# Two MoE layers: rows sorted by expert through DRAM and multiplied in fixed blocks of 128, in place of every listed expert over every row

## What is computed

```python
x = x + 0.5 * L0_ffn(layernorm(x))     # an adapter picked for each sequence
x = x + L0_attn(layernorm(x))
x = x + 0.5 * L0_ffn(layernorm(x))
x = x + 0.5 * L1_ffn(layernorm(x))     # MoE, the first
x = x + L1_attn(layernorm(x))          # selective scan
x = x + 0.5 * L1_ffn(layernorm(x))     # MoE, the second
```

```python
scores = sigmoid(xf @ gate_w + bias)
top_scores, top_idx = top_k(scores, 2)
top_scores = top_scores / (top_scores.sum(-1) + 1e-6)
w = zeros((T, 8)); w[t, top_idx] += top_scores
hact = gelu(einsum('th,ehi->tei', xf, up_w) + up_b)
eo = einsum('tei,eih->teh', hact, down_w) + down_b
combined = einsum('teh,te->th', eo * 0.1, w)
shared = (gelu(xf @ sw_up + sb_up) @ sw_down + sb_down) * 0.1
out = shared + combined
out = out / (max(abs(out), -1) + 1e-6)
```

## Time and profile before

| | |
|---|---|
| median of 3 runs | 1553.57 us (1551.65 to 1554.36) |
| the profiled execution, its own time | 1552.47 us |
| its span in the trace | 1550.7 us |
| PE busy | 1394.1 us, 90% |
| DVE / ACT / POOL busy | 947.5 / 801.6 / 400.0 us |
| mean granted clock of TensorE | 0.946 of 2.4 GHz |
| first MoE layer, from its first instruction to the barrier behind it | 664.1 to 965.5 us |
| second MoE layer, from its first instruction to the end | 1260.0 to 1550.7 us |

### The profile page before, as it was taken

One profiled execution on the slowest core, in us unless ns is written; L12 is line 12 of the kernel. 1 busy time (PEld: TensorE's weight loads), 2 busy tenths in 40 slices (PEclk: granted clock), 3 DMA queues, 4 the chain that ended last, 5 costly groups with the idle time before them and its releaser, 6 DMA issues. The chain is left out here.

```text
span 1550.7 us, 22874 instructions
## 1 busy us (share of the span) xinstructions
PE 1394.1 (90%) x7314; PEld 729.1 (47%) x7314; DVE 947.5 (61%) x1896; ACT 801.6 (52%) x1465; POOL 400.0 (26%) x585
## 2 busy tenths in 40 slices
PE   2896899999999879799999997899998779999997
PEld 1672222222222257567777764122221157777776
DVE  5677688889889347451222256699899941222236
ACT  0220688888888714354343354665666444443432
POOL 4021232322330012220000002788888710000000
PEclk9996799999999979889999998799999979999999
DMA  4020121222211010000000000444444300000001
GB/s 94 0 83 1 62 73 52 63 72 72 79 66 43 1 19 1 1 16 1 17 16 1 17 1 23 159 157 140 146 133 154 111 1 16 16 15 2 16 14 42
DMA packets 81206, 77.31 MB, mean 50 GB/s; under 512 B 21004, under 2 KB 60376, under 8 KB 81112
## 3 DMA queue, kind: packets, MB, share of 16 engines
q1 hardware_dynamic: 78992, 75.85, 15.7%
q10 hardware_dynamic: 2120, 0.28, 0.2%
HBM read 55.78 MB, written 16.78 MB: 47 GB/s over the span
## 5 line engine op out<-in xcount | busy, mean ns | idle before, releaser
L1375 ACT ACTIVATE m_hidden<-m_pU,m_up_b 128x512 f32<-128x512 f32 x320 | 219.8, 687 | 265.6 <-PE m_pU L1524 265.4
L1183 DVE TENSOR_REDUCE at_nm<-at_mx 128x2 f32<-128x1024 f32 x256 | 303.8, 1219 | 40.4 <-PE at_mx L1026 39.0
L1531 PEld LDWEIGHTS m_pD<-m_down,m_hidden 128*128 128x128 f32 x2560 | 296.7, 192 | 32.5 <-issue 32.5
L1531 PE MATMUL m_pD<-m_down,m_hidden 128*128 128x128 f32 x2560 | 297.1, 275 | 0.0
L1129 ACT ACTIVATE at_probs<-at_ring 128x512 f32<-128x512 f32 x512 | 269.2, 605 | 47.3 <-PE at_ring L1038 45.8
L1524 PE MATMUL m_pU<-m_xT_all,m_up 128*128 128x512 f32 x640 | 291.2, 601 | 1.1 <-PEq L305 0.5
L1500 DVE TENSOR_TENSOR m_out_b<-m_pD,m_down_b 128x512 f32<-128x512 f32 x64 | 44.2, 691 | 288.6 <-PE m_pD L1531 288.6
L1524 PEld LDWEIGHTS m_pU<-m_xT_all,m_up 128*128 128x128 f32 x640 | 118.0, 193 | 123.7 <-issue 123.5
L2023 POOL TENSOR_TENSOR ss_hc<-ss_h,ss_c_all 128x512 f32<-128x512 f32 x128 | 161.9, 1271 | 52.1 <-DVE ss_h L2195 44.6
L1038 PE MATMUL at_ring<-at_qq,at_kk 51*128 51x512 bf16 x512 | 163.3, 386 | 7.1 <-ACT at_probs L1129 6.1
L1026 PE MATMUL at_mx<-at_kk,at_qq 48*128 48x512 bf16 x512 | 156.0, 398 | 12.7 <-DVE at_nm L1183 8.1
(11 more groups left out here) (282 smaller groups left out, 1511.1 us busy)
## 6 DMA issues: line engine op xcount, KB each, us to landing
ss_dtb<-ss_dt_rows SPq DMA_DIRECT2D x128, 256.0 KB
at_qq<-q_stack SPq DMA_DIRECT2D x64, 96.0 KB, 2.3
at_kk<-k_stack SPq DMA_DIRECT2D x64, 96.0 KB, 2.3
q_stack<-at_qs SPq DMA_DIRECT2D x8, 384.0 KB, 2.6
k_stack<-at_ks SPq DMA_DIRECT2D x8, 384.0 KB, 3.0
ss_stack<-ss_parts SPq DMA_DIRECT2D x96, 32.0 KB, 2.7
X<-in_L_attn_x_dram SPq DMA_DIRECT2D x8, 256.0 KB, 6.1
q_stack<-at_qs SPq DMA_DIRECT2D x8, 256.0 KB, 2.9
```

The costliest lines, as they stand in the source:

```text
L1183: dve.tensor_reduce(nm[group % 2][:, 2 * (pair % 2) + parity, 2 * half:2 * half + 2], mx[parity][:, :, :], AX.X, ALU.max, negate=True).the ...
L1375: act.activation(hidden[t % 2][:, k, :], pU[k][:, :], ACT.Gelu, bias=up_b[buf][:, k:k + 1]).then_inc(s.gelu_done, 1)
L1531: last = pe.matmul(pD[t % 2][:, c, :], hidden[t % 2][:, k, c * P:(c + 1) * P], down[buf][:, k, :], start=(k == 0), stop=(k == NI - 1))
```

## The change

In each MoE layer the shared expert stays as it is. The listed experts go. In their place:

- **Routing.** The chain (now 37 links) gives each of the 8192 pairs a place in a list sorted by half of the sequences (0 to 3, 4 to 7), then by expert, each expert's part padded to a multiple of 128 rows. PE counts with two products after the shared expert's second up product. `index` holds the places, `expert_of` the expert of each block.
- **Scatter.** ACT keeps all normalised rows of the layer in `mw_rows` (130 words: the row, its id, its weight). POOL writes them to DRAM (`sorted_rows`) with indirect DMAs, 128 rows of 520 bytes each: 16 for each half and each choice k, 64 in a layer. Between the choices it waits until the first has landed and sets the id and weight of the other (`mark`).
- **Blocks.** 39 blocks of 128 rows for each half, 78 in a layer, whatever the routing (4096 pairs of a half and at most 8 x 127 of padding). SP loads a block to `xb` (8 buffers). PE transposes it (`turn`), ACT copies the transpose to SBUF (`take_turned`), DVE copies the up weights of the block's expert from `up_all` into one of two fixed places (`take_up`), PE makes four products of 128 columns (`block_up`), ACT four Gelus of 128 columns, PE four products for the down part with weights addressed by a register (`block_down`), DVE adds the bias, multiplies by the row's weight and converts the row ids. POOL writes the 128 results with an indirect DMA (`put`) to `pair_rows` in DRAM, 78 in a layer; padding rows have an id out of bounds and are skipped.
- **Finish.** SP reads both results of a sequence back, DVE adds them to `acc` (now the same memory as `m_xT_all`) and finishes as before. The first half's four sequences are finished during the second half's blocks, in five pieces each from block 47 on (`FINISH_AT`, `PIECES`); the other four after the last block.
- All 8 experts' weights are loaded at the start of the layer (16 DMAs, 4 MB). Each engine that addresses by expert loads the block's expert number into a register (`expert_at`), once a block. Early in the kernel, SP fills both sorted lists in DRAM with empty rows (`fill_sorted`, two DMAs of 9984 rows of 520 bytes). A barrier pair with a clearing of semaphores stands between the first MoE layer and the scan, in addition.

The core of the diff (new sides, with what the text below speaks of):

```diff
+HALVES = 2
+ID, WEIGHT = D, D + 1
+PAIR_ROWS = 2 * NB * L
+HB = (2 * HT * P + E1 * (P - 1)) // P
+TB = HALVES * HB
+X_BUFS, Y_BUFS, T_BUFS = 8, 12, 3
+LEAD_AT = {14: 3, 19: 4, 22: 5, 25: 6, 28: 7, 36: 8, 38: 9}
+SILU_AT = 23
+def fill_sorted(sp, r):
+    sp.wait_ge(r.made, 2)
+    for rows in r.sorted:
+        sp.dma_start(rows.rearrange("(j p) d -> p j d", p=P), r.empty[:, :].unsqueeze(1).broadcast_to([P, TB, ROW])
+                     ).then_inc(r.filled, 16)
...
+            def load_block(j):
+                if j >= X_BUFS:
+                    sp.wait_ge(s.y_ready, j - X_BUFS + 1)
+                sp.dma_start(xb[:, j % X_BUFS, :], sorted_rows[j * P:(j + 1) * P, :]).then_inc(xb_in[j % X_BUFS], 16)
+            def wait_written(blocks):
+                for i in range(Y_BUFS):
+                    sp.wait_ge(y_out[i], 16 * len(range(i, blocks, Y_BUFS)))
...
+            for e in range(E1):
+                sp.dma_start(up_all[:, e, :], ins["L1_ffn_up_w"][e]).then_inc(s.experts_in, 16)
+                sp.dma_start(down_all[:, e, :, :], ins["L1_ffn_down_w"][e].rearrange("(k i) h -> i k h", i=P)
+                             ).then_inc(s.experts_in, 16)
+            sp.wait_ge(s.list_ready, 1)
+            for half in range(HALVES):
+                for k in range(2):
+                    sp.wait_ge(scattered[half][k], 16 * HT)
+                for j in range(HB):
+                    load_block(half * HB + j)
+                    if half and j in Y_LOAD_AT:
+                        if j == min(Y_LOAD_AT):
+                            wait_written(HB)
+                        for b in Y_LOAD_AT[j]:
+                            load_results(b)
+            if lead is not None:
+                scan_lead_stores(sp, lead)
...
+            def mark(half, k):
+                tiles = slice(half * HT, (half + 1) * HT)
+                pool.tensor_copy(v.rows[:, tiles, ID:ROW], v.idw[:, k, tiles, :]).then_inc(s.marked, 1)
+                pool.wait_ge(s.marked, 2 * half + k + 1)
+            def scatter(half, k, t):
+                at_tile = half * HT + t
+                pool.indirect_dma_start(sorted_rows, bass.IndirectOffsetOnAxis(ap=index[:, k, at_tile:at_tile + 1], axis=0),
+                                        v.rows[:, at_tile, :], None, bounds_check=TB * P - 1, oob_is_err=False
+                                        ).then_inc(scattered[half][k], 16)
+            def put(j):
+                pool.wait_ge(s.y_ready, j + 1)
+                pool.indirect_dma_start(pair_rows, bass.IndirectOffsetOnAxis(ap=y_id[j % Y_BUFS][:, :], axis=0),
+                                        y[j % Y_BUFS][:, :], None, bounds_check=PAIR_ROWS - 1, oob_is_err=False
+                                        ).then_inc(y_out[j % Y_BUFS], 16)
+            pool.wait_ge(s.weighted, 1)
+            mark(0, 0)
+            pool.wait_ge(s.placed, 1)
+            for t in range(HT):
+                scatter(0, 0, t)
+            pool.wait_ge(scattered[0][0], 16 * HT)
+            mark(0, 1)
+            for t in range(HT):
+                scatter(0, 1, t)
+            mark(1, 0)
+            for t in range(HT):
+                scatter(1, 0, t)
+            pool.wait_ge(scattered[1][0], 16 * HT)
+            mark(1, 1)
+            for j in range(HB):
+                if j < HT:
+                    scatter(1, 1, j)
+                put(j)
+            for j in range(HB):
...
+            def take_turned(j):
+                act.wait_ge(s.turned, j + 1)
+                if j >= T_BUFS:
+                    act.wait_ge(s.bup_done, j - T_BUFS + 1)
+                act.copy(xT[j % T_BUFS], pU[2 + j % 2][:, 0:P]).then_inc(s.xT_taken, 1)
+            def gelus(j, e):
+                if j >= T_BUFS:
+                    act.wait_ge(s.bdown_done, j - T_BUFS + 1)
+                act.wait_ge(s.bup_done, j + 1)
+                for k in range(NI):
+                    act.activation(hid[j % T_BUFS][:, k, :], pU[j % 2][:, k * P:(k + 1) * P], ACT.Gelu,
+                                   bias=v.up_b[:, bass.ds(e, 1), k:k + 1].rearrange("p a b -> p (a b)")
+                                   ).then_inc(s.hid_done, 1)
+            for j in range(TB):
+                after = expert_at(act, j + 1) if j + 1 < TB else None
+                gelus(j, e)
+                e = after
+                if j + 2 < TB:
+                    take_turned(j + 2)
+                if lead is not None and j - HB in LEAD_AT:
+                    scan_lead_act(act, g, q=ahead, s=lead, t=LEAD_AT[j - HB])
...
+            def finish(b, piece):
+                tiles = slice(b * NC, (b + 1) * NC)
+                if piece == 0:
                     norm.begin(b)
+                    dve.wait_ge(y_in[b % 2], 32 * (b // 2 + 1))
+                    norm.link(dve.tensor_tensor(acc[:, tiles, :], acc[:, tiles, :], yb[b % 2][:, 0, :, :], ALU.add))
+                if piece == 1:
+                    dve.tensor_tensor(acc[:, tiles, :], acc[:, tiles, :], yb[b % 2][:, 1, :, :], ALU.add
+                                      ).then_inc(s.y_added, 1)
+                    dve.wait_ge(s.y_added, b + 1)
+                if piece == 2:
                     norm.link(dve.tensor_reduce(most[:, tiles], acc[:, tiles, :], AX.X, ALU.max,
...
+            def take_up(j, e):
+                if j > 1:
+                    dve.wait_ge(s.bup_done, j - 1)
+                dve.tensor_copy(up_now[j % 2], up_all[:, bass.ds(e, 1), :].rearrange("d a i -> d (a i)")
+                                ).then_inc(s.up_ready, 1)
+            for j in range(TB):
+                if j + 2 < TB:
+                    further = expert_at(dve, j + 2)
+                    take_up(j + 2, further)
+                if j >= Y_BUFS:
+                    dve.wait_ge(y_out[j % Y_BUFS], 16 * (j // Y_BUFS))
+                dve.wait_ge(xb_in[j % X_BUFS], 16 * (j // X_BUFS + 1))
+                dve.tensor_copy(y_id[j % Y_BUFS][:, :], xb[:, j % X_BUFS, ID:ID + 1])
+                dve.wait_ge(s.bdown_done, j + 1)
+                dve.tensor_tensor(yt[j % 2][:, :], pD[j % 2][:, 0, :],
+                                  v.down_b[:, bass.ds(e, 1), :].rearrange("p a d -> p (a d)"), ALU.add
+                                  ).then_inc(s.y_taken, 1)
+                dve.wait_ge(s.y_taken, j + 1)
+                dve.tensor_scalar(y[j % Y_BUFS][:, :], yt[j % 2][:, :], xb[:, j % X_BUFS, WEIGHT:ROW], None, ALU.mult
+                                  ).then_inc(s.y_ready, 1)
+                e, after = after, further
+                jj = j - HB - FINISH_AT
+                if 0 <= jj < HS * PIECES:
...
+            def turn(j):
+                pe.wait_ge(xb_in[j % X_BUFS], 16 * (j // X_BUFS + 1))
+                if j > 1:
+                    pe.wait_ge(s.xT_taken, j - 1)
+                pe.transpose(pU[2 + j % 2][:, 0:P], xb[:, j % X_BUFS, 0:D], g.identf[:, :]).then_inc(s.turned, 1)
+            def block_up(j):
+                pe.wait_ge(s.up_ready, j + 1)
+                pe.wait_ge(s.xT_taken, j + 1)
+                if j > 1:
+                    pe.wait_ge(s.hid_done, NI * (j - 1))
+                for k in range(NI):
+                    last = pe.matmul(pU[j % 2][:, k * P:(k + 1) * P], up_now[j % 2][:, k * P:(k + 1) * P],
+                                     xT[j % T_BUFS], start=True, stop=True)
+                last.then_inc(s.bup_done, 1)
+            def block_down(j, e):
+                pe.wait_ge(s.hid_done, NI * (j + 1))
+                if j > 1:
+                    pe.wait_ge(s.y_taken, j - 1)
+                for k in range(NI):
+                    last = pe.matmul(pD[j % 2][:, 0, :], hid[j % T_BUFS][:, k, :],
+                                     down_all[:, bass.ds(e, 1), k, :].rearrange("i a d -> i (a d)"),
+                                     start=(k == 0), stop=(k == NI - 1))
+                last.then_inc(s.bdown_done, 1)
+            pe.wait_ge(s.experts_in, EXPERT_LOADS)
+            pe.wait_ge(s.list_ready, 1)
+            pe.wait_ge(s.gelu_done, NI * NB)
+            pe.wait_ge(s.shared_acc, NB)
+            e = expert_at(pe, 0)
+            turn(0)
+            turn(1)
+            block_up(0)
+            for j in range(TB):
+                if j + 2 < TB:
...
+            nc.all_engine_barrier()
+            nc.clear_and_free_semaphores(taken_once)
+            nc.all_engine_barrier()
```

592 lines of the change are left out of this document (318 added, 274 removed).

## The result

The changed kernel took 1512.6 us (1509.7 to 1520.4), the kernel before 1553.4 beside it: ratio 0.9746, 95% interval 0.9706 to 0.9787. The prediction was 1514. The profiled execution spans 1508.1 us against 1550.7.

A forecast was written before the change was run, and what follows sets the result against it. PE's columns in the listed experts were taken as the bound. First layer -22.5 us, second -24.6, less added costs, made -40 from 1552.5: 1512.5, and 1.1 more against the median, 1514; range 1460 to 1600.

The forecast's parts named there:

- the terms added at the end of the sum: Outside the layers' sums: second barrier pair 3 us, PE idle then below full clock 1.5 a layer, added constants 1.
- The shared expert, ended at 58: Start of each MoE layer: the shared expert still ends 58 us after the layer's start; PE's routing wait next to nothing.
- POOL's DMA, c = 1.2: POOL's scatters: each indirect DMA costs c = 1.2 us, 32 precede the first block, which starts at 64.4 us.
- the formula: First block starts at 26 + 32c us after the layer's start; the buffer stall adds 48c, together 80 us per us of c.
- The round, 2.1: Each block's round takes 2.1 us, near PE's floor of 1.96; 78 rounds make 164 us a layer.
- finish, 12 us in blocks 47 to 66: Finish pieces on DVE lengthen rounds to 2.9, 2.9 and 3.5 us: 3.0 a sequence, 12 for four, PE waiting for up weights.
- The stall for buffers, 1 us: Block 27 waits for result 15's buffer, held by POOL's scatters: 57.6 against 56.7, so 1 us lost at c = 1.2.
- The lead, 10.5, in the first layer: The scan's start, mixed into the first layer's listed experts, costs 10.5 us there, as before the change.
- The tail, 7 us to the first sum: After the last block: last result, DMA, landing and reading back 7 us, then four sequences 15 us, 19 in the first layer.
- The fills, at nothing: Early in the kernel, two DRAM fills take all DMA engines 61 us but are covered; uncovered they would cost up to 30.
- The rival of the lock: In rounds, DVE's copy waits 0.6 us for POOL's put in 57%: round 2.4, 1561 us; within the long-round rival's 0.13.
- POOL as the bound: Rival, chance 0.26: slower, as start and buffers cost 80 us a layer per us of c over 1.2; 1578 at 1.6.

The follow-up runs named there:

- r9: The changed kernel itself, run again unedited on a held-back chip: 1603.6 us, ratio 1.034.
- e10: Changed kernel with POOL waiting for the landing of each of the 48 scatters ahead of the first put; on the chip of r9: 1733.5 us.
- e1: Changed kernel without DVE's copy of a block's up weights (output not the reference's), on a clean chip: 1490.4 us.
- e6: Changed kernel with DVE loading the expert number into its register one round earlier, on a clean chip: 1502.2 us.
- c1: Changed kernel with 18 result buffers, DVE's register load one round ahead and the lead's stores behind the last reading back; on the chip of r9: 1594.4 us.
- e4: Changed kernel with 18 buffers for results instead of 12, on a clean chip: 1501.8 us.
- e7: Changed kernel with SP issuing the scan lead's stores behind the reading back of the last four sequences, on a held-back chip: 1609.0 us.
- c2: Changed kernel with c1's edits (14 buffers) and, in the first layer, POOL clearing a tile before scatters and the first 39 blocks' puts; clean chip: 1539.7 us.

## Why the prediction was right, and where its steps were not

The number is right on the chips that do not hold PE back, and there partly by luck. The first layer gained 11.5 us where 22.5 were predicted, the second 27.7 where 24.6 were, and the rest of the kernel gained 3.4 where the terms added at the end of the sum were to cost 7. These errors of 11, 3 and 10 us cancel to 2.5. That the result came to such a chip was luck as well: on the chip of r9 the same prediction is wrong. The main path is as predicted: what is saved is PE's columns, and the first block and the blocks' rounds take their time from POOL's issues and from PE.

- **The shared expert, ended at 58.** It ended at 60.9 and 61.1. The two counting products, put at nothing, hold PE for 1.8 us (671.50 to 673.33), and the up products ahead of them took 1.0 longer than before (9.78 against 8.81). This is hidden: the first block comes later still.
- **POOL's DMA, c = 1.2.** 1.275 (0.97 and 0.30 to the next). Shown by POOL's timeline. The first block's transpose came at 66.3 after the start, predicted 64.4; with the c of the trace the formula gives 66.8, and it held within 2.1 us in the first layers at 1.68 and 3.05 (3.7 in e10's second); on a held-back chip at 1.275 it does not hold, 91.3 us in r9. The Trainium skill's "DMA: Bandwidth & Descriptors", "Anatomy of one DMA — SWDGE (gpsimd) path", with 2.0 us for each and most of it landing, stands: a put lands 2.3 us after its issue in the median, and issues follow one another sooner.
- **The round, 2.1.** Too long: 1.89 to 1.90, even under the floor of 1.96. Sixteen half products at 0.112 are right (0.89 and 0.90), but a transpose holds PE for 0.11, not 0.17. On PE the register load and the address steps are hidden altogether, and e1 shows that the copy is too. Rounds 4 to 22 of the second layer have a mean of 1.96 all the same, and 1.90 both in e6 and in e1, so DVE's load and copy together cost some 0.06. In all this gave 11 to 16 us a layer (78 x 0.14 to 78 x 0.2).
- **finish, 12 us in blocks 47 to 66.** Right in the second layer: 2.97, 2.57 and 3.04 are 2.9 over three quiet rounds, 11.5 for four sequences. e6 and e1 show the mechanism: the pieces delay the register load and the copy behind it. With the load moved away (e6, c1) 2.0 of these 2.9 remain, which are the pieces themselves.
- **The stall for buffers, 1 us.** Too small: 6.5 and 6.4. The mechanism was right and the size was not. The inputs account for more than was missing: 48 x 0.075 = 3.6 for c, and blocks that are 0.2 us shorter each reach block 27 some 5.4 us earlier, which gives 10 where 6.5 were waited. So the formula overshoots by 3.5. e4 removed the stall.
- **The lead, 10.5, in the first layer.** Here a step failed: 78 blocks took 184.6 us, first to last transpose, and in the second layer 165.1. Of the 19.5 between them 10.5 were predicted. Some 3 to 4 more are statistics, which I had put into the tail alone: for the first two sequences, where a variance of seven small operations follows them, the rounds are 3.88 and 3.92 us where the second layer has 1.90, and PE waits 1.72 and 1.31 us in them for the copy behind. Those of the other two (0.94 each) fall into rounds in which PE does not wait for DVE. The other 16 or so are the lead itself, half as much again as priced: rounds of 4.47, 3.96, 4.66, 5.72 and 5.85 stand where the second layer has 2.99, 1.97, 2.98, 1.97 and 1.90. In the longest PE waits for ACT's Gelus, which stand behind eight of the lead's operations and two table loads (887.42 to 895.05):

```profile
896.35 2.07 PE L1753 MATMUL m_pD<-m_down_all,m_hidden 128*128 x8 [2.82 <-ACT m_hidden L1531]
```

The POOL work of the lead adds to it at the end. DVE's and POOL's timelines of the kernel after:

```profile
906.20 2.00 DVE L1667 COPY m_up<-m_up_all 128x512 f32 x1 [0.46 <-issue]
...
908.50 1.99 DVE L1688 TENSOR_SCALAR m_y<-m_yt,m_xb 128x128 f32<-128x128 f32 x1
```

```profile
906.62 1.28 POOL L1926 TENSOR_TENSOR ss_corr<-ss_nd,ss_rw 128x512 f32<-128x512 f32 x1
908.07 1.01 POOL L1478 DMA_INDIRECT pair_rows<-m_y,m_y_id  x1 [0.17 <-issue]
909.10 1.29 POOL L1931 TENSOR_TENSOR ss_dt<-ss_lnw,ss_corr 128x512 f32<-128x512 f32 x1
```

- **The tail, 7 us to the first sum.** From the start of the last `y` 6.9 in the second layer, 11.0 in the first, since SP issues the lead's stores first; e7 shows 2.6 of the 4. The four sequences took 3.84 each, and 4.80 with statistics, as predicted.

```profile
914.25 13.00 SPq L1915 DMA_DIRECT2D ss_stack<-ss_parts  x12
927.68 5.48 SPq L1421 DMA_DIRECT2D m_hidden<-pair_rows  x6
```

- **The fills, at nothing.** SP issued both from 33.8 to 57.8 us, they landed 45.4 us after their issue in the median (the profile page's DMA issues), and the attention's first stack went out at 87.1 us (87.5 before). The cover held.
- **The rival of the lock.** The Trainium skill, "SBUF — State Buffer", section "Who interferes with whom", would have a float32 copy on DVE and the writing of descriptors for a GpSimd DMA exclude each other. In the second layer's blocks the copy is 0.43 us in the median and 0.65 at most, and POOL's 77 DMAs are 0.97 in the median and 1.46 at most: next to nothing beside descriptors, where the page has 620 against 3100 ns (in its section "A bandwidth-pool intuition that's wrong (but worth ruling out)", not in the one that the prediction names). Where it shows, the copy begins in one of two short stretches of a DMA: begun 0.57 to 0.74 us behind its start, 13 copies took 0.48 to 0.65; and of those begun within 0.2 us of its start, three come with a DMA of 1.44 to 1.46 and four with one of 1.14 to 1.17, where the rest have 0.97. Beside POOL's two-input tensor operations DVE's copy took 2.00 (above), so that half of the rule the trace does show.
- **POOL as the bound.** It came true in c2; in e10, at 3.05, it is mixed with the gaps of a held-back chip. At 1.68, with puts spaced too, the first layer lost more than its gain: 35.8 us over the kernel after, with the mends in it, where 80 us a layer for each microsecond of c makes 32.
- **What the prediction did not have** is the held-back chip: a time of 1603.6, slower than before and outside the range. That the gaps go with dense indirect DMAs is shown by e10 and by the puts of r9; by what way POOL's DMAs reach PE, ACT and DVE is open, and so is why only some chips do it. Every run here has a recorded span and clock, so whether the recording has a part in it is not tested either. Two things speak against PE's clock as the cause: ACT is held as well, and in e7 the gaps begin at full clock, as this stretch of it shows (2.96 of 4 us busy, clock 1.00):

```profile
700.00:704.00 4.00, 2.96 (x11) 1.71 (x10) 0.00 (x0) 0.00 (x0) 2.15 (x3) 1.00 0.15 50
```

## What to carry to other kernels

When rows are moved by an engine's own DMAs, count its issues ahead of the first block and its results' buffers as one formula in the period, and read the period first: here the start of the first block and the stall for results' buffers went by it. Put a register load where its engine waits anyway, not between a long pass and the operation that another engine needs. And time such a kernel on several chips before keeping it: the ratio was 0.975 on one and 1.034 on another.

## What the runs showed of the hardware

- An indirect DMA of 128 rows of 512 or 520 bytes holds POOL for 0.97 us, the next follows 0.30 later, and a small clearing (0.13) fits into that; it lands 2.1 to 4.5 us after its issue, 2.3 in the median.
- Two of the chips held PE, ACT and DVE back while POOL issued such DMAs every 1.275 us, and not at 1.90 (r9) or 3.05 (e10); PE then starts matmuls 0.7 us apart, an ACT instruction comes up to 24 us late, and POOL is not slowed. The kernel before, whose POOL issues none, took the same time beside every one of them (medians 1553.0 to 1553.5).
- A DVE copy or scale of 0.3 to 0.4 us beside a two-input POOL operation of 1.28 took up to 2.00.
- Three products of 512 columns with the identity took 5.5 us on a PE that had been idle (granted clock 0.50), 2.9 later on (0.99).
